# Routed experts of a mixture layer: 24 of 39 tiles in pairs of one expert, with the first layer transposed

## The reference

```
x = x + tanh(g_xattn) * cross_attention(layernorm(x), ctx)          # 16 heads of 64
x = x + tanh(g_ffn)   * moe(layernorm(x))

moe(xf):                               # xf: 2048 tokens x 256
  sh     = gelu(xf @ sw1[s] + sb1[s])  # 2 shared experts, hidden 512
  shared = (sum_s sh @ sw2[s] + sb2.sum(0)) / 2
  gates  = xf @ router_w + router_b    # 8 experts
  topv, topi = top_k(gates, 2);  probs = softmax(topv)
  h  = gelu(xf @ w1[e] + b1[e])        # w1[e]: 256 x 512
  ye = h @ w2[e] + b2[e]               # w2[e]: 512 x 256
  return shared + sum over the two chosen e of probs * ye
```

## Time and profile before

| | us |
|---|---|
| median of 3 runs (lowest to highest) | 387.39 (387.09 to 388.18) |
| the profiled execution | 387.97 |
| its span | 386.1 |
| PE busy | 379.8 |
| DVE / ACT / POOL busy | 280.9 / 249.4 / 221.1 |

### The profile page before, as it was taken

One profiled execution on the slowest core, in us unless ns is written; L12 is line 12 of the kernel. 1 busy time (PEld: TensorE's weight loads), 2 busy tenths in 40 slices (PEclk: granted clock), 3 DMA queues, 4 the chain that ended last, 5 costly groups with the idle time before them and its releaser, 6 DMA issues.

```text
span 386.1 us, 9097 instructions
## 1 busy us (share of the span) xinstructions
PE 379.8 (98%) x2725; PEld 354.3 (92%) x2726; DVE 280.9 (73%) x627; ACT 249.4 (65%) x600; POOL 221.1 (57%) x261
## 2 busy tenths in 40 slices
PE   8999999999999999999999999999999999999996
PEld 7898989999999899999999989999999999999995
DVE  5798799988988998797889885445554455445386
ACT  2766545646755635888869757776667666777850
POOL 8366656788788762577872345555555555552200
PEclk9999999999999999999999999999999999999999
DMA  7990000001000066003930112222222222221397
GB/s 230 306 321 3 2 14 29 16 22 33 14 14 27 17 230 247 14 4 70 274 98 1 36 49 70 83 70 83 69 82 73 78 71 79 75 75 42 87 355 254
DMA packets 32539, 35.89 MB, mean 93 GB/s; under 512 B 9531, under 2 KB 26365, under 8 KB 32509
## 3 DMA queue, kind: packets, MB, share of 16 engines
q1 hardware_dynamic: 27664, 25.21, 21.9%
q0 software_dynamic: 4768, 10.28, 8.7%
q10 hardware_dynamic: 76, 0.02, 0.0%
HBM read 25.79 MB, written 9.59 MB: 92 GB/s over the span
## 4 chain that ended last, share of the span: by engine, by line
PE 92%; DVE 3%; POOL 2%; ACT 1%; issue 1%; DVEq 0%; POOLq 0%
PE psum L1348 14%; PE psum L1395 13%; PE psum L1206 12%; PE psum L1229 11%; PE psum L1166 10%; PE psum L1122 9%; PE psum L1414 4%; PE psum L1089 3%; PE psum L1337 2%; PE psum L1008 2%; PE psum L1046 2%; PE psum L1070 2%; PE psum L1154 1%; PE psum L988 1%; PE psum L1186 1%
## 5 line engine op out<-in xcount | busy, mean ns | idle before, releaser
L1883 DVE COPY hs<-psum 128x512 f32<-128x512 f32 x39 | 27.0, 691 | 56.4 <-PE psum L1395 56.4
L681 POOL DMA_INDIRECT xsl<-y_rows,table x39 | 38.3, 982 | 47.5 <-PE psum L1337 36.2
L688 POOL DMA_INDIRECT y_tok<-ysl,table x39 | 38.6, 990 | 31.8 <-ACT ysl L949 31.5
L966 ACT ACTIVATE hr<-psum,b_cur 128x128 f32<-128x128 f32 x156 | 44.4, 372 | 3.0 <-DVE hr_lo L1873 1.2
L662 POOL DMA_INDIRECT names<-named,pos x32 | 37.8, 1181 | 12.8 <-issue 7.9
L949 ACT ACTIVATE ysl<-psum,table 128x256 f32<-128x256 f32 x39 | 18.5, 475 | 38.7 <-PE psum L1348 38.7
L615 POOL TENSOR_TENSOR Eb<-Eb,rinv 128x512 f32<-128x512 f32 x32 | 33.5, 1065 | 13.1 <-DVE rinv L1604 13.1
L825 ACT ACTIVATE yTb<-psum 128x256 f32<-128x256 f32 x16 | 6.2, 385 | 42.6 <-PE psum L1186 42.6
L1348 PE MATMUL psum<-w_hi,hr_hi 128*128 x156 | 28.0, 301 | 0.0
L1873 DVE TENSOR_TENSOR hr_lo<-hr,hr_hi 128x512 fp32r<-128x512 f32 x39 | 26.6, 682 | 1.8 <-ACT hr_hi L970 1.8
L1395 PE MATMUL psum<-w_hi,xsT_hi 128*128 x78 | 27.6, 436 | 0.0
(11 more groups left out here) (248 smaller groups left out, 1169.7 us busy)
## 6 DMA issues: line engine op xcount, KB each, us to landing
w_raw<-in_L_ffn_w SPq DMA_DIRECT2D x2, 4096.0 KB, 18.1
y_got<-y_tok SPq DMA_DIRECT2D x8, 512.0 KB, 7.6
xs_all<-in_x SPq DMA_DIRECT2D x4, 512.0 KB, 12.3
sw_raw<-in_L_ffn_sw SPq DMA_DIRECT2D x2, 1024.0 KB, 13.9
y_rows<-ybuf SPq DMA_DIRECT2D x16, 128.0 KB, 1.7
out<-xs_all SPq DMA_DIRECT2D x3, 512.0 KB, 3.2
wq_sb<-in_L_xattn_Wq SPq DMA_DIRECT2D x2, 512.0 KB, 6.5
wo_sb<-in_L_xattn_Wo SPq DMA_DIRECT2D x1, 1024.0 KB, 14.2
```

What stands on the lines that cost most here:

```text
L681: nc.gpsimd.indirect_dma_start(xsl[:, s % 2, :], None, y_rows, bass.IndirectOffsetOnAxis(ap=table[:, s, 0:1].bitcast(I32), axis=0)).then_i ...
L688: nc.gpsimd.indirect_dma_start(y_tok, bass.IndirectOffsetOnAxis(ap=table[:, s, 1:2].bitcast(I32), axis=0), ysl[:, s % 2, :], None).then_in ...
L966: last = nc.scalar.activation(hr[:, m, :], bank[4 + par][:, m * P:(m + 1) * P], ACT.Gelu, bias=b1_cur[:, par, m:m + 1])
```

## The change

Of the 39 slot tiles, 24 become 12 pairs ("doubles"), both tiles of one expert; the order is 6 single tiles, 12 pairs, 9 single tiles. DVE's routing chain computes places for both lists (`entry(s)` maps a step to its place).

- A pair's rows are transposed together, 256 columns wide. Its first layer has w1 stationary and the 256 rows moving, in 24 matmuls, so the result comes out transposed; the copy `hs` and its four transposes a tile fall away. ACT applies gelu straight from PSUM, in two halves of the hidden size through a single buffer `hr2`.
- The weights of the pair's expert are first copied by DVE to a fixed place, `w1_cur[par]`, high and low part, 128 x 1024 words each (`move_weights`).
- `w1_cur` lies where the low part of the shared weights was. SP therefore saves that (2 MB) to DRAM in front of the routed stage and loads it back in four pieces during steps 35 to 38 of its table loop; PE waits for it ahead of the late shared sub-blocks.
- Gathers of pairs alternate between `xsl` and a second buffer `xsl2`, three pairs ahead. POOL's gathers and scatters are ordered by pairs.
- Some semaphores are merged, without another order.

The core of the diff, shortened:

```diff
+DOUBLES = (TOK * TOPK // P - E) // 2
+DOUBLE0 = 6
+SINGLE1 = DOUBLE0 + 2 * DOUBLES
+        w1_cur = at_words("w1_cur", [P, 2, 2, KD, HID], AT_SW + 2 * SW_WORDS, F32R)
...
 @block.sync
+            sp.wait_ge(sw_ready, SW_PIECES)
+            sp.dma_start(sw_lo_kept[:, :], sw_s[1][:, :].bitcast(F32)).then_inc(sw_moved, 16)
...
+                n = s - (SLOT_TILES - BACK)
+                if n >= 0:
+                    sp.wait_ge(h_psum, SINGLE1 + n)
+                    piece = slice(n * 2 * SW_WORDS // BACK, (n + 1) * 2 * SW_WORDS // BACK)
+                    sp.dma_start(sw_s[1][:, piece].bitcast(F32), sw_lo_kept[:, piece]).then_inc(sw_moved, 16)
 @block.gpsimd
+            for d in range(1, DOUBLES):
+                for n in range(2):
+                    scatter(tile_of(d - 1) + n)
+                if d + 3 < DOUBLES:
+                    for n in range(2):
+                        gather(tile_of(d + 3) + n)
...
 @block.scalar
+            def double(d, par, s, j):
+                def gelus(h):
+                    act.wait_ge(h_psum, s + (h + 1))
+                    act.wait_ge(ht_lo, s + h)
+                    for m in range(2):
+                        last = nc.scalar.activation(hr2[:, m, :], bank[2 + 2 * par + h][...], ACT.Gelu, bias=...)
+                    last.then_inc(ht_raw, 1)
+                def kept(h):
+                    act.wait_ge(ht_raw, s + (h + 1))
...
+                    nc.scalar.activation(hr2_hi[:, 2 * h:2 * h + 2, :], hr2[:, :, :], ACT.Copy).then_inc(ht_hi, 1)
+                act.wait_ge(b1_ready, s + 2)
+                gelus(0)
+                turned_wide(s + 2, 1 - par)
+                kept(0)
+                gelus(1)
+                kept(1)
+                output(s - 2, 0)
+                output(s - 1, 1)
 @block.tensor
+            def give_wide(s, n):
+                e = expert(n)
+                pe.wait_ge(ye_ready, s)
+                for h in range(2):
+                    pe.wait_ge(ht_lo, s + (h + 1))
+                    for t in range(2):
...
+                        if h == 1:
+                            last.then_inc(ye_psum, 1)
+                    if h == 0:
+                        last.then_inc(half_used, 2)
+            def double(d, par, s, j):
+                pe.wait_ge(xt_lo, s + 2)
...
+                pe.wait_ge(w1_moved, s + (2 - DOUBLE0))
+                for m in range(HC):
+                    n, half = 0, m // 2
+                    for x_part, w_part in ((xsT2_hi, 0), (xsT2_hi, 1), (xsT2_lo, 0)):
+                        for k in range(KD):
+                            last = nc.tensor.matmul(bank[2 + 2 * par + half][...],
+                                                    w1_cur[:, par, w_part, k, m * P:(m + 1) * P],
+                                                    x_part[:, k, :], start=(n == 0), stop=(n == 3 * KD - 1))
+                            n += 1
+                    if m % 2 == 1:
+                        last.then_inc(h_psum, 1)
...
 @block.vector
-            link(nc.vector.tensor_copy(run_e[0][:, PADE:], tiles_e[:, :]))
...
+            link(nc.vector.tensor_copy(run_e[0][:, 0, PADE:], tiles_e[:, :]))
+            link(nc.vector.tensor_reduce(run_e[0][:, 1, PADE:], full_tile[:, :, 1::2], AX.X, ALU.add))
...
+            parts = ((slice(0, SINGLES), ends_s[:, 0:E - 1]), (slice(SINGLES, SLOT_TILES), in_pairs[...]))
...
+            def move_weights(par, n):
+                nc.vector.tensor_copy(w1_cur[:, par, n, :, :], w1_s[n][:, at(expert(2 + par)), :, :]...bitcast(F32)
+                                      ).then_inc(w1_moved, 1)
...
+            def double(d, par, s, j):
+                if d == 0:
+                    hidden_left(DOUBLE0 - 1, 1)
+                dve.wait_ge(ht_raw, s - (1 if d == 0 else 2))
+                bias_of(2 + par, par).then_inc(b1_ready, 2)
+                turned_wide(s + 2, 1 - par)
+                if d == 0:
+                    move_weights(1, 1)
+                half_left(0)
+                if more:
+                    dve.wait_ge(h_psum, s + 2)
+                    move_weights(par, 0)
+                half_left(1)
+                if more:
+                    move_weights(par, 1)
```

More of the change, by code:

```diff
@@ L58 @@
 IN_FLIGHT = 4
+BACK = 4
 COPIES = 3
@@ L367, in turn_of, with entry, tile_of, wide @@
             return c - len(LATER)
[L371 to L374, removed]
+        assert DOUBLE0 % 2 == 0 and DOUBLES % 2 == 0 and 2 < DOUBLE0 < SINGLES
+        def entry(s):
+            return s if s < DOUBLE0 else s + SINGLES - DOUBLE0 if s < SINGLE1 else s - 2 * DOUBLES
+        def tile_of(d):
+            return 2 * d + DOUBLE0
+        def wide(d):
+            return 2 <= d < DOUBLES and d % 2 == 0
+        HS_TURNS = DOUBLE0
         def experts(eng):
             regs = [eng.alloc_register(f"expert{n}") for n in range(IN_FLIGHT)]
[L380 to L388, removed]
+            def fetch(n, q):
+                eng.load(regs[n % IN_FLIGHT], emap[0:1, at(q)])
+            return (lambda n: eng.snap(regs[n % IN_FLIGHT], min_val=0, max_val=E - 1)), fetch
+        def routed(eng, step, double, before={}):
+            for s in range(DOUBLE0):
                 if s in before:
                     before[s]()
[L391 to L396, removed]
+                step(s, s % 2)
+            double(0, 0, tile_of(0), 0)
+            with eng.Fori(0, DOUBLES // 2 - 2) as j:
+                for u in range(2):
+                    double(None, 1 - u, j * 4 + tile_of(1 + u), j)
+            for d in range(DOUBLES - 3, DOUBLES):
+                double(d, d % 2, tile_of(d), (d - 1) // 2)
+            for s in range(SINGLE1, SLOT_TILES):
+                step(s, s % 2)
         LAST = NSUB - 1
@@ L481, in _ @@
                     sp.wait_ge(xt_psum, s - IN_FLIGHT + 1)
-                sp.load(regs[n], name_tile[0:1, s:s + 1])
+                sp.load(regs[n], name_tile[0:1, entry(s):entry(s) + 1])
                 row = sp.snap(regs[n], min_val=0, max_val=NAME_TILES - 1)
@@ L974, in _ @@
             w2_copy(0)
-            routed(act, step)
+            routed(act, step, double)
             output(SLOT_TILES - 2, SLOT_TILES % 2)
@@ L1421, in _ @@
             pe.wait_ge(sh_raw, EARLY * PAIRS)
-            routed(pe, step)
+            routed(pe, step, double)
             give(SLOT_TILES - 2, SLOT_TILES % 2, SLOT_TILES - 2)
+            pe.wait_ge(sw_moved, 16 + 16 * BACK)
             hidden(EARLY, late, range(0, 1))
@@ new lines, in _ @@
+            link(nc.vector.tensor_scalar(unused[:, 0, :], tiles_e[:, :], -1.0, float(NT), ALU.mult, ALU.add))
+            link(nc.vector.tensor_tensor(unused[:, 0, 0:E - 1], unused[:, 0, 0:E - 1], two_u[:, 1:E], ALU.add))
+            parts = ((slice(0, SINGLES), ends_s[:, 0:E - 1]), (slice(SINGLES, SLOT_TILES), in_pairs[:, PADE:PADE + E - 1]))
+            for part, stops in parts:
+                size = part.stop - part.start
+                link(nc.vector.tensor_tensor(passed[:, part, :], iota_slot[:, part].unsqueeze(2).broadcast_to([P, size, E - 1]),
+                                             stops.unsqueeze(1).broadcast_to([P, size, E - 1]), ALU.is_ge))
@@ L1807, in _ @@
             link(nc.vector.tensor_reduce(emap_f[:, :], passed[:, :, :], AX.X, ALU.add))
             link(nc.vector.tensor_copy(emap[:, :], emap_f[:, :]))
-            link(nc.vector.tensor_scalar(unused[:, :], tiles_e[:, :], -1.0, float(NT), ALU.mult, ALU.add))
-            link(nc.vector.tensor_tensor(moved[:, :, :], passed[:, :, :],
-                                         unused[:, 0:E - 1].unsqueeze(1).broadcast_to([P, SLOT_TILES, E - 1]), ALU.mult))
+            for n, (part, _) in enumerate(parts):
+                size = part.stop - part.start
+                link(nc.vector.tensor_tensor(moved[:, part, :], passed[:, part, :],
+                                             unused[:, n, 0:E - 1].unsqueeze(1).broadcast_to([P, size, E - 1]), ALU.mult))
@@ L1901, in _ @@
             w2_rest(7)
-            routed(dve, step, {1: lambda: w2_rest(0), 2: late_start})
+            routed(dve, step, double, {1: lambda: w2_rest(0), 2: late_start})
             hidden_left(SLOT_TILES - 1, (SLOT_TILES - 1) % 2)
```

270 lines of the change are left out of this document (207 added, 63 removed).

## The result

The changed kernel takes 391.94 us at the median against 387.32 for the kernel before on the same chip, a ratio of 1.0125 (95% interval 1.0089 to 1.0162). These are five runs from 390.75 to 394.18 us, without a sixth in a slower state (397.35), which would make the median 392.7, the number that the texts put on record ahead of the experiments compare with. The forecast was 380.8 with a range to 385.3: the sign is wrong and the range does not hold the time. The runs of before lie within 1.2 us. The profiled execution took 391.94 (span 390.2).

A forecast was written before the change was run, and what follows sets the result against it. TensorE was taken as the bound, by throughput (busy 379.8 of 386.1 us). 9.1 saved in pairs less 0.9 entry, 1.2 exit and 0.4 routing gave 6.6 us: 381.4 profiled, 380.8 median, range 378.4 to 385.3.

The forecast's parts named there:

- PE's pair: TensorE's work per pair of tiles: 6.20 us instead of 6.96, 0.76 saved, 9.1 us over 12 pairs.
- The others in the pairs: ACT, DVE and POOL keep the 6.20 us pace inside pairs, with 0.9 us of slack on POOL as thinnest cover.
- the 1.2 that I took from L1830: DVE's weight copy of 1024 words, put at 1.2 us from a subtraction of that size; 0.7 was the cheap end.
- T: The end of a pair's first layer on PE, from which the prediction counts the other engines' times.
- (a): Rival in the pairs: stalls recur as DVE copies and indirect DMAs stretch each other, 383.7 us; chance 0.17.
- (b): Rival in the pairs: that collision on all four indirect DMAs, 412 us at worst; chance 0.07 with other slower ways.
- whichever rate: In the pairs: by the skill's contention rule the DVE copies would collide with GpSimd at any copy rate.
- Entry: From step 5 into the first pairs: loss 0.9 us, 0.3 with copies of 0.7 us, at most 2.
- Exit: Steps 30 and 31 after the pairs: loss 1.2 us, between 0.6 and 2.
- The schedule that I wrote down for a pair: POOL in a pair: scatters at T+5.0 and 6.3, gathers at 7.5 and 8.8, landed T+11.6, wanted T+12.5.
- Transfers: Saving the 2 MB `sw_lo` costs nothing; loading it back in four pieces from steps 30 to 33 costs 0, at most 1.
- Routing and w2: DVE's longer routing chain makes w2's load 1.8 us late, its conversion starts at 200.3; loss 0.4, 0 to 1.5.

The follow-up runs named there:

- entry order alone: Changed kernel with pair 3's gathers before tile 4's scatter and pair 1's second weight copy before pair 0's remainder of x: 392.81 us (1.011).
- split turn: Changed kernel with entry and exit queue orders altered, reload four steps later, and tile 7 turned after tile 3's second layer: 383.77 us (0.9884).
- the best version: Kernel with altered entry and exit orders, later reload and later turn of tile 7, plus six tables in flight instead of four: 383.12 us (0.9885).

## Why the prediction was wrong

**PE's pair: right.** 6.19 us for 6.20, 0.77 saved instead of 0.76. The form of 256 columns costs what L1206 showed, and twice the weight loads cost nothing.

**The others in the pairs: right in the result, two sizes wrong.** The groups of the kernel after:

```profile
L2096 DVE CAST w_cur<-w_lo 128x1024 fp32r x12 | 8.6, 716 | 0.0
L2096 DVE CAST w_cur<-w_hi 128x1024 fp32r x12 | 8.4, 704 | 0.0
L1077 ACT ACTIVATE hr_hi<-hr 128x512 fp32r<-128x512 f32 x24 | 15.2, 632 | 4.8 <-PE psum L1493 3.9
L2135 DVE TENSOR_TENSOR hr_lo<-hr,hr_hi 128x512 fp32r<-128x512 f32 x24 | 16.6, 692 | 16.8 <-ACT hr_hi L1077 16.8
```

The copy of 1024 words takes 0.71 us, not the 1.2 that I took from L1830: the cheap end. The Trainium skill's "VectorE: DVE Perf Modes", the perf-mode tier table, made it an estimated 0.7, and this trace agrees, also for a cast to fp32r. The half copies and remainders are 512 words and not 256 (0.63 and 0.69 where I put 0.4). For DVE the errors cancel nearly, and pairs 4 to 10 show no wait. ACT's outputs come later by them: with T at 290.58 POOL's first scatter starts at 296.25 and the second gather at 300.10, T+5.7 and T+9.5 instead of T+5.0 and T+8.8. Landed 2.8 later it is at T+12.3, and PE wants it at T+12.5: 0.2 us of slack, not 0.9.

**Rivals (a) and (b): false for this time.** POOL's starts in pairs 4 to 10 are 1.27 to 1.30 us apart where nothing is waited for, and its 23 gathers between 240 and 318 us take 946 to 1379 ns, median 972. The Trainium skill's "GPSIMD Engine Reference", Key points, has the two engines contend. Here that hangs on when the copy starts:

```profile
268.70 1.38 POOL L732 DMA_INDIRECT xsl<-y_rows,table  x1 [0.30 <-issue]
269.16 0.69 DVE L2096 CAST w_cur<-w_hi 128x1024 fp32r x1
...
275.34 0.96 POOL L732 DMA_INDIRECT xsl<-y_rows,table  x1 [0.30 <-issue]
275.35 0.72 DVE L2096 CAST w_cur<-w_hi 128x1024 fp32r x1
```

The two gathers above 1.1 us (1.14 and 1.38) are those in which a copy starts 0.2 and 0.5 us after them, and both end some 0.24 us behind the copy; where the two start together, as here from 275 us on, the gather keeps its 0.96. No pair from 4 on is moved by it in this trace. In two others (entry order alone, split turn) pair 5 takes 6.69 and 6.63 us: a gather of the rows that it turns started 0.05 us behind a copy and took 1.48 and 1.47. That is as far as (a) was seen. The prediction's "whichever rate" goes beyond the page's words, which name two-port modes and two inputs; the copies ran at the double rate, so nothing here tests it. I gave these two most of what I had against the forecast, and they hold none of the loss.

**Entry: 3.0 us instead of 0.9 (at most 2).** The DVE queue was named, 0.9 (0.87 here, and the wait is for `w_cur`). Not named: step 5 needs tile 7's rows one step after their buffer came free, so a landing of 2.8 us or more shows (1.2 here, up to 2.5), and POOL's queue in pairs 2 and 3 (0.9). The order edit took back 0.42 of that, in pair 2; for pair 3 the queue is read from the timelines and not tested.

**Exit: the step that failed.** The sum has 1.2 for it, from the order of PE, ACT and DVE; POOL's order at the exit was never walked through. The schedule that I wrote down for a pair gives the loss when it is put there: scatters at T+5.0 and T+6.3 behind the outputs, the gather at T+7.5, landed at T+10.3. In the pairs that is wanted two pairs on, at T+12.5. Tile 30's is wanted one pair on, at T+6.2: 4.1 us late, and 4.68 was measured. I had every number and checked the repeating part alone. With the clock behind it (not in the sum at all) this is 6.8 us, more than the whole gain that I forecast.

**Transfers: "0, at most 1" was 2.5.** I asked whether the reload meets gathers with cover; it met scatters, whose buffers ACT needs in the same step. Even without it and with the gathers in time, steps 30 and 31 lose 2.3 us, not 1.2: `give_wide(28)` waits 0.87 for `ysl` where I had 0.3, and step 31 takes 3.25 where 1.97 would do.

**Routing and w2: nothing instead of 0.4.** The load of w2 is issued 2.1 us later than before (178.31, 176.24), near the 1.8 of the forecast, but its 4 MB took 19.2 us instead of 22.3. So its conversion starts at 197.48 and not at 200.3, and PE waits for nothing there. Why the load was faster is not shown.

**In all** the edges cost 13.3 us where the sum has 2.1, and w2 0 where it has 0.4: 10.8 us more than forecast. From 381.4 for the profiled execution that gives 392.2, against 391.94. The mechanism of the pair holds; with the orders and a transfer moved it brings 4.9 of the 9.1 us by the medians (383.12 against 387.99), 4.3 by the stage (132.5 against 136.7). What still separates the best version from 127.6 us in this stage is 1.4 in step 5, 1.2 in pairs 0 to 3 and 2.3 at steps 30 and 31. Why the gather of tile 7 lands after 2.9 us in one execution and 4.8 in another stays open. So does what the copies by themselves cost: a pair that reads its weights in place, without them, was not run.

## What to carry to other kernels

When a loop's form changes in the middle, the repeating part is the easy half: write the queue of every engine, the one that issues DMAs above all, across both seams, and ask of each load at the seam when it is wanted, since its distance in steps changes there. A load whose buffer is free should not stand in a queue behind a store that waits for a result. A wait of several microseconds on TensorE is to be priced with the slow clock behind it, and shorter ones can bring it too.

## What the runs showed of the hardware

- After TensorE stood 4.7 us, the granted clock was 0.56 over the next 5.1 us, couples of 256-column matmuls 0.43 us apart instead of 0.24; with filler in the wait it stayed at 1.00.
- After two waits of 0.57 and 1.61 us in one step the granted clock was 0.66 over the next 5.06 us; after 0.57 and 1.68 in another kernel it stayed at 1.00.
- The same gather, with the same instructions ahead of it, landed 2.9 us after its issue in one execution and 4.8 us in another.
- The scatter of tile 26 (128 rows) held its buffer for 4.9 us with a 512 KB load issued 0.3 us behind it, in a stretch that moved 185 GB/s in all, and for 2.7 us at most in the kernel without the load.
- A gather's issue on POOL took 0.96 us when a copy of 1024 words on DVE started with it, 1.14 and 1.38 us when the copy started 0.2 and 0.5 us after it, and 1.48 us when it had started 0.05 us before.
